# Latent attention in a two-layer decoder: the 64-row second part of the query products on two halves of TensorE's rows

## The reference

```python
q_latent = hidden_states @ Wqa                  # 256 -> 192
q = (q_latent @ Wqb).reshape(b, s, 16, 128)     # 64 plain + 64 rotary columns a head
q_pe, k_pe = rope(q_pe), rope(k_pe)
kv = (c_kv @ Wkvb)                              # c_kv has 64 columns
scores = einsum('bhqd,bhkd->bhqk', q_full, k_full) * scale   # causal
out = (softmax(scores) @ v) @ Wo
```

## Time and profile before

| | us |
|---|---|
| median of 3 runs | 822.75 (818.8 to 828.49) |
| the profiled execution | 815.32 |
| its span | 813.4 |
| PE busy | 623.1 (77%) |
| DVE busy | 469.7 (58%) |
| ACT busy | 320.4 (39%) |
| POOL busy | 254.9 (31%) |
| share of PE in the chain that ended last | 63% |
| mean granted TensorE clock | 0.88 |

### The profile page before, as it was taken

How to read it: one execution, slowest core, us unless ns; L and a number is a source line. 1 busy time by engine, 2 the same in 40 slices (tenths; PEclk the granted TensorE clock), 3 DMA queues, 4 the chain that set the end, 5 groups by cost and what they waited for, 6 DMA issues and landing times.

```text
span 813.4 us, 13142 instructions
## 1 busy us (share of the span) xinstructions
PE 623.1 (77%) x4335; PEld 435.4 (54%) x4338; DVE 469.7 (58%) x988; ACT 320.4 (39%) x754; POOL 254.9 (31%) x258
## 2 busy tenths in 40 slices
PE   3808899253099999999588998999988777763674
PEld 3408444142078888898473465556576356542332
DVE  4696699956445545555155153442546845878675
ACT  1501500242224333334242373553746435564444
POOL 3380178746500000000343892754903320100000
PEclk9958999755589999999868999999999878995778
DMA  9841000445541111110540000000000400000000
GB/s 321 293 161 47 1 0 1 155 155 179 192 135 41 52 52 52 52 40 26 162 125 0 1 1 0 0 0 0 0 2 1 155 1 2 2 2 1 6 19 26
DMA packets 35589, 50.01 MB, mean 61 GB/s; under 512 B 3288, under 2 KB 26400, under 8 KB 35296
## 3 DMA queue, kind: packets, MB, share of 16 engines
q1 hardware_dynamic: 33024, 41.39, 15.8%
q0 software_dynamic: 2528, 8.13, 2.7%
HBM read 38.50 MB, written 11.01 MB: 61 GB/s over the span
## 4 chain that ended last, share of the span: by engine, by line
PE 63%; DVE 18%; ACT 9%; POOL 4%; issue 3%; DMA 2%; SPq 0%; ACTq 0%; DVEq 0%; POOLq 0%
PE bank L1482 15%; PE bank L1495 5%; PE bank L1599 4%; PE bank L1598 4%; PE bank L1653 4%; POOL sorted_rows L472 3%; PE bank L1620 3%; DVE qk L898 2%; ACT sm L680 2%; PE bank L1370 2%; PE bank L1413 2%; PE bank L1414 2%; PE bank L1415 2%; PE bank L1612 2%; PE bank L1901 2%
## 5 line engine op out<-in xcount | busy, mean ns | idle before, releaser
L635 ACT ACTIVATE hf<-bank,be 128x256 f32<-128x256 f32 x120 | 50.4, 471 | 86.6 <-PE bank L1482 72.5
L1482 PE MATMUL bank<-h,wsp 128*128 128x256 f16 x720 | 81.3, 273 | 2.0 <-DVE h L1050 1.4
L1482 PEld LDWEIGHTS bank<-h,wsp 128*128 x720 | 69.5, 98 | 12.1 <-issue 3.7
L478 POOL DMA_INDIRECT yg<-expert_rows,pos x16 | 15.6, 977 | 185.8 <-DMA expert_rows<-yb 181.3
L1048 DVE CAST h<-hf 128x512 f16<-128x512 f32 x60 | 25.6, 427 | 65.2 <-ACT hf L635 63.7
L550 ACT CAST wsp<-wraw 128x2048 f16<-128x2048 f32 x12 | 22.6, 1897 | 73.0 <-DMA wraw<-in_L_ffn_W 73.0
L1151 DVE SCALAR_TENSOR_TENSOR sm<-bank,const 128x512 f32<-128x512 f32 x32 | 22.1, 692 | 50.1 <-PE bank L1620 50.1
L680 ACT ACTIVATE sm<-sm,nm 128x128 f32<-128x128 f32 x128 | 49.7, 393 | 1.0 <-DVE nm L1154 1.0
L460 POOL TENSOR_TENSOR kvp<-xnT,cxT 128x512 f32<-128x512 f32 x32 | 34.9, 1112 | 48.2 <-DVE xnT L877 40.2
L444 POOL TENSOR_TENSOR wsp<-wraw,wsp 128x2048 f16<-128x2048 f32 x10 | 40.9, 4095 | 10.8 <-ACT wsp L550 10.5
L488 POOL TENSOR_TENSOR rq<-qs,const 128x256 f32<-128x256 f32 x32 | 23.3, 728 | 65.2 <-ACT qs L686 65.1
(11 more groups left out here) (302 smaller groups left out, 1424.8 us busy)
## 6 DMA issues: line engine op xcount, KB each, us to landing
wraw<-in_L_ffn_W SPq DMA_DIRECT2D x16, 512.0 KB, 4.3
wraw<-in_L_ffn_W SPq DMA_DIRECT2D x8, 1024.0 KB, 5.5
sorted_rows<-early POOLq DMA_DIRECT2D x2, 1920.0 KB, 14.1
xg<-sorted_rows SPq DMA_DIRECT2D x15, 256.0 KB, 2.8
expert_rows<-yb SPq DMA_DIRECT2D x15, 256.0 KB, 2.2
tapR<-in_kpad SPq DMA_DIRECT2D x16, 128.0 KB, 6.9
x<-in_x SPq DMA_DIRECT2D x1, 1024.0 KB, 5.9
cx<-in_ctx SPq DMA_DIRECT2D x1, 1024.0 KB, 10.3
```

What stands on the lines that cost most here:

```text
L635: last = nc.scalar.activation(hf[:, p, SLOTS * k:SLOTS * k + SLOTS], bank[2 * (layer - 1) + p][:, SLOTS * k:SLOTS * k + SLOTS], ACT.Gelu, ...
L1482: last = nc.tensor.matmul(b[:, SLOTS * (f % 2):SLOTS * (f % 2) + SLOTS], w[a_][:, c, P * f:P * f + P], inp[:, b_, c, :], start=(c == 0 and ...
```

## The change

The second part of a query product (rows 128 to 192 of Wqb, 64 of TensorE's rows) is no longer made group by group. The latents' second half is computed twice over, into both halves of the partitions: `Wqa`'s last 64 columns are given twice by the host, `wqa` is 256 columns wide, and `ql1` has 128 partitions. The weights `wqb[:, 1]` hold the even groups in partitions 0 to 63 and the odd groups in 64 to 127. `queries_low` issues the 64-row products of two neighbouring groups one behind the other, on the two halves of the rows and into banks 1 and 2; they open the accumulation. `queries_high` issues the 128-row product of one group, which closes it and signals ACT. In the loop, step j now issues `queries_high` of group j-1, in odd steps preceded by `queries_low` of groups j-1 and j; group 7 is closed after the last scores. ACT's order, DVE's and POOL's are as before. The preparation follows the new places of the weights, and one more DMA brings them.

```diff
-        wqa = sb("wqa", [P, DC, QL], F32, s4w)
+        wqa = sb("wqa", [P, DC, 2 * P], F32, s4w)
...
-        ql1 = sb("ql1", [64, 2, P], F32, s4)
+        ql1 = sb("ql1", [P, 2, P], F32, s4)
...
-            sp.dma_start(wqb[0:64, 1].rearrange("p h n -> p (h n)"), a["L1_attn_Wqb"][P:QL, :]).then_inc(sem("w4_loaded"), 16)
+            for k in range(2):
+                sp.dma_start(wqb[64 * k:64 * k + 64, 1].rearrange("p (g two h) n -> p g two (h n)", two=2, h=4)[:, :, k],
+                             a["L1_attn_Wqb"][P:QL, :].rearrange("p (g two n) -> p g two n", two=2, n=4 * P)[:, :, k]).then_inc(sem("w4_loaded"), 16)
...
-                nc.scalar.copy(ql1[:].rearrange("p u s -> p (u s)"), bank[0][0:64, 2 * P:4 * P]).then_inc(sem("lat_copied"), 1)
+                nc.scalar.copy(ql1[:].rearrange("p u s -> p (u s)"), bank[0][:, 2 * P:4 * P]).then_inc(sem("lat_copied"), 1)
...
             for k in range(2):
+                half = slice(64 * k, 64 * k + 64)
                 for j in range(8):
-                    last = nc.tensor.transpose(bank[k][0:64, 64 * j:64 * j + 64], wqb[0:64, 1, 8 * k + j, 0:64], i64)
+                    last = nc.tensor.transpose(bank[k][0:64, 64 * j:64 * j + 64], wqb[half, 1, 8 * (j // 4) + 4 * k + j % 4, 0:64], ident[half, half])
...
-                for dst, w in ((bank[0][:, 0:2 * P], wqa[:, :, 0:P]), (bank[0][0:64, 2 * P:4 * P], wqa[:, :, P:QL])):
+                for dst, w in ((bank[0][:, 0:2 * P], wqa[:, :, 0:P]), (bank[0][:, 2 * P:4 * P], wqa[:, :, P:2 * P])):
...
-            def queries(i, j):
-                u, g = j // 4, j % 4
-                hs = slice(4 * g, 4 * g + 4)
+            def queries_low(i, j):
+
+                u = j // 4
                 if j == 0:
                     pe.wait_ge(sem("lat_copied"), i + 1)
-                pe.wait_ge(sem("q4_copied"), i * 8 + (j + 1))
-                nc.tensor.matmul(bank[1 + g % 2][:], ql0[:, u, :], wqb[:, 0, hs, :].rearrange("p h n -> p (h n)"), start=True, stop=False)
-                nc.tensor.matmul(bank[1 + g % 2][:], ql1[:, u, :], wqb[0:64, 1, hs, :].rearrange("p h n -> p (h n)"), start=False, stop=True).then_inc(sem("q4_psum"), 1)
+                pe.wait_ge(sem("q4_copied"), i * 8 + (j + 2))
+                for k in range(2):
+                    g, rows = (j + k) % 4, slice(64 * k, 64 * k + 64)
+                    nc.tensor.matmul(bank[1 + k][:], ql1[rows, u, :], wqb[rows, 1, 4 * g:4 * g + 4, :].rearrange("p h n -> p (h n)"), start=True, stop=False)
+
+            def queries_high(i, j):
+                u, g = j // 4, j % 4
+                nc.tensor.matmul(bank[1 + g % 2][:], ql0[:, u, :], wqb[:, 0, 4 * g:4 * g + 4, :].rearrange("p h n -> p (h n)"), start=False, stop=True).then_inc(sem("q4_psum"), 1)
...
                     scores(i, (j - 1) // 4, (j - 1) % 4)
                     if after is not None:
-                        if j == 1:
-                            queries(after, 0)
-                        queries(after, j)
+                        if j % 2:
+                            queries_low(after, j - 1)
+                        queries_high(after, j - 1)
                     if j >= 4:
                         turn_p(i, 0, j - 4)
                 scores(i, 1, 3)
+                if after is not None:
+                    queries_high(after, 7)
                 turn_p(i, 1, 0)
...
             latents(0)
-            queries(0, 0)
+            queries_low(0, 0)
+            queries_high(0, 0)
             key_latents(0, 0)
-            queries(0, 1)
+            queries_high(0, 1)
             turn_kv(0, 0)
-            for j in range(2, 5):
-                queries(0, j)
+            queries_low(0, 2)
+            queries_high(0, 2)
+            queries_high(0, 3)
+            queries_low(0, 4)
+            queries_high(0, 4)
             pe.wait_ge(sem("kvr_ready"), 1)
             key_latents(0, 1)
-            queries(0, 5)
+            queries_high(0, 5)
             turn_kv(0, 1)
-            for j in range(6, 8):
-                queries(0, j)
+            queries_low(0, 6)
+            queries_high(0, 6)
+            queries_high(0, 7)
...
+    wqa = inputs["L1_attn_Wqa"]
+    host["L1_attn_Wqa"] = np.ascontiguousarray(np.concatenate([wqa, wqa[:, P:]], 1))
```

More of the change, by code:

```diff
@@ L321, in prep4_moves @@
             for k in range(2):
-                yield wqbT[:, 8 * k:8 * k + 8, P:QL], bank[k][0:64, :].rearrange("p (h n) -> p h n", h=8)
+                yield (wqbT[:, :, P:QL].rearrange("p (g two h) n -> p g two h n", two=2, h=4)[:, :, k],
+                       bank[k][0:64, :].rearrange("p (g h n) -> p g h n", g=2, h=4))
             for k in range(2):
@@ L325, in prep4_moves @@
             for k in range(2):
-                yield wqb[0:64, 1, 8 * k:8 * k + 8, 0:64], bank[4 + k][0:64, :].rearrange("p (h n) -> p h n", h=8)
+                yield (wqb[64 * k:64 * k + 64, 1].rearrange("p (g two h) n -> p g two h n", two=2, h=4)[:, :, k, :, 0:64],
+                       bank[4 + k][64 * k:64 * k + 64, :].rearrange("p (g h n) -> p g h n", g=2, h=4))
             for k in range(4):
@@ L1523, in _ @@
             pe.wait_ge(sem("y_ready"), ET + CREDIT)
-            pe.wait_ge(sem("w4_loaded"), 96)
+            pe.wait_ge(sem("w4_loaded"), 112)
             def prep_copied(n):
@@ L1545, in _ @@
             for k in range(2):
+                half = slice(64 * k, 64 * k + 64)
                 for j in range(8):
-                    last = nc.tensor.transpose(bank[k][0:64, 64 * j:64 * j + 64], wqb[0:64, 1, 8 * k + j, 0:64], i64)
+                    last = nc.tensor.transpose(bank[k][0:64, 64 * j:64 * j + 64], wqb[half, 1, 8 * (j // 4) + 4 * k + j % 4, 0:64], ident[half, half])
                 last.then_inc(sem("prep4_psum"), 1)
             prep_copied(10)
[L1550 to L1555, removed]
+            for k in range(2):
+                for j in range(8):
+                    h = 8 * k + j
+                    last = nc.tensor.matmul(bank[2 + k][:, 64 * j:64 * j + 64], wqbT[:, h, 0:P], wkT[:, h, :], start=True, stop=True)
+                last.then_inc(sem("prep4_psum"), 1)
+            for k in range(2):
+                for j in range(8):
+                    h = 8 * (j // 4) + 4 * k + j % 4
+                    last = nc.tensor.matmul(bank[4 + k][64 * k:64 * k + 64, 64 * j:64 * j + 64], wqbT[:, h, P:QL], wkT[:, h, :], start=True, stop=True)
+                last.then_inc(sem("prep4_psum"), 1)
             pe.wait_ge(sem("wo4b_loaded"), 16)
```

## The result

The changed kernel takes **879.57 us** (median of 4 runs, 878.01 to 880.29) against 820.77 for the kernel before (4 runs, 818.58 to 828.49, the three of the prediction and one more beside the changed kernel): a ratio of 1.0707, 95% interval 1.0657 to 1.0756, some 58.8 us slower. The profiled execution took 879.73 us with a span of 877.8, which is 64.4 more than the span of 813.4 before.

The account below looks back on a forecast made before the run. PE was taken to bound the kernel, busy 46.1 of 48.35 us a pass. Waits +38, opening -3 and clock +20 made +55 on 815.3, 870.3; with a third of the distance to the median's 877.8, 873 us (846 to 896).

Parts of the forecast that it names:

- The waits, +38: Three loop passes: PE waits for ACT's copies, 2.87 us before turn_p in steps 4 to 7; +12.65 us a pass.
- The clock, +20: Loop passes: granted clock falls to 0.78 because of PE's waits, +6.8 us a pass.
- The sign that I had set, passes of 61 to 69 us: Loop passes: a pass of 61 to 69 us would show the forecast right, under 48 us wrong.
- The waits come, but the clock holds: Rival, loop passes: same waits without a lower clock, 850 to 858 us; chance 15%.
- The opening, -3: Opening of the latent attention: no exponentials there, so pairing gains; -3 us (-5 to -2).
- The pair at 0.86 plus switches: Two 64-row products side by side: 0.86 us, 1.25 with entry and exit in place of 2.40; 1.15 saved per pair.
- one by one: Rival, 64-row pairs: halves do not run side by side, 0.86 us more each, +13.8, 887 us; chance 5%.
- half an overlap: Rival, 64-row pairs: second product starts with the first's second pass, 1.29 us a pair, +7, 880 us; chance 8%.
- PE stays the bound: Rival, wait for qT at L1627: ACT copies qT(j) before qs(j-1) is ready; POOL caps the gain, 803 to 811 us; 6%.
- The preparation at "nothing": Preparation: one more DMA and eight 64-row transposes on the other half of the rows, costed at nothing.
- The base: Whole kernel before: profiled execution of 815.3 us, to which the terms were added; median 822.75 us, 7.4 higher.

Follow-up runs that it names:

- experiment 4: Changed kernel with ACT's exponentials of group j-2 put before its copy of the query products, PE untouched: 821.1 us, ratio 1.0116 to the kernel before.
- experiment 5: Changed kernel with added products whose result nobody uses filling PE's waits in steps 4 to 7: 850.4 us, ratio 1.0494 to the kernel before.
- experiment 3: Changed kernel with ACT's copy of the query products one step later, behind the next qT copy, PE untouched: 811.6 us, ratio 1.0016 to the kernel before.
- experiment 6: Kernel of experiment 2 with both 64-row products of a pair on partitions 0 to 63: 811.9 us, ratio 1.0007 to the kernel before.
- experiment 2: Changed kernel with PE's query products in the loop one step earlier, pairing kept: 801.6 us, ratio 0.9898 to the kernel before; repeated, 799.6 us, 0.9863.
- Experiment 8: Changed kernel with all 64-row weight transposes from rows 0 to 63: 870.1 us, ratio 1.0737 to the kernel before; beside it the changed kernel unedited, 867.7 us.
- The second group of runs: Changed kernel, unedited, timed again beside the kernel before on another chip: 867.7 us, ratio 1.0688.

## Why the prediction was right

It was 873 us (range 846 to 896, slower by more than 1% at 0.91), and the median is 879.57. Mechanism and place were right, not only the number; the size of the clock term was in part luck. Step by step:

- **The waits, +38.** Right in place, releaser and size. 2.87 us before turn_p was worked out and 2.79 is there; 2.43 before the scores of step 4 against 2.26, and 0.88 in steps 2 and 3 against 0.73. In all that is 14.9 us of waits in a pass (11.2 + 3.7), where 15.7 was put. To part waits from clock, I take PE's busy time at full clock from experiment 4: 42.64 + 42.64 + 40.82 = 126.1 in three passes. The changed kernel's is 148.2, so the clock cost it 22.1, and at full clock its passes would take, by this estimate, 204.1 - 22.1 = 182.0, that is +39.1. The second profile of the same kernel (passes of 210.5, PE busy 154.9) gives 210.5 - 28.8 = 181.7, +38.8. Forecast: 180.9. The passes of experiment 5, at 0.97 to 1.00, are 183.7 in all.
- **The clock, +20.** 22.1 and 28.8 in the two profiles, and some 16 by the ratios of experiment 5, whose clock of 0.97 is not quite whole in two of three passes. The level was nearly right: 0.78 was forecast for the stretch from the first scores to the last copy of query products, and the three passes of the first profile have 0.92, 0.76 and 0.85 there. The stretch takes 43.1, 49.0 and 45.6 us, where 39.8 + 6.8 was forecast. Whole passes, in both profiles, have 0.80 to 0.92. It is also the term that differs most between executions of one kernel: 0.92 and 0.85 in the first pass. That the sum fits so well owes something to luck. The forecast took the level of one other stretch, with waits of 1.98 us and 0.78, and experiment 3 shows that such waits do not fix it: up to 2.04 us, at 1.00, 0.97 and 0.93. The sign that I had set, passes of 61 to 69 us, held for two of the three (66.0, 71.8, 66.3). "The waits come, but the clock holds" is what experiment 4 looks like, with waits of 1.25, near the 1.23 that stood at a full clock in the earlier trace rows.
- **The opening, -3.** -3.0 measured.
- **The pair at 0.86 plus switches.** 1.06 to the product behind it and 0.19 more in that product, 1.07 in the chain against 0.88 without a pair ahead of it: 1.25, as forecast. The rivals "one by one" and "half an overlap" both fall with experiment 6: 1.91 is what one by one looks like, and half an overlap would be 1.29 and the switch. The Trainium skill ("TensorE: Matmul & The Clock Gate", Part 3, The mechanism) has matmuls start and end strictly in program order, and has those on different rows of the array overlap. The trace agrees with the overlap and does not contradict the order: the four records of the pair on two halves, in experiment 6, start in rising order, two by two, and end at 515.06, 515.07, 515.49 and 515.50. My prediction went wrong where it drew 1.29 from that rule and then set the trace against it; which record belongs to which product the trace does not say.
- **PE stays the bound.** Its place was right but its condition was not met. Moved a step (experiment 2) it comes true: POOL, named there, is indeed the next limit, and it caps the pass at 45.9, a gain of 2.4; up to 3 was forecast.
- **The preparation at "nothing".** In the first profile it was +12.7. Experiment 8 finds it in no other profile, the changed kernel's second one included, so the step stands; the cause of the 12.7 stays open.
- **The end of the kernel, not in the sum.** -6.0, with the clock at 0.85 in place of 0.80. In the profiles of the experiments this same code stands at 0.79 to 0.85 and takes 158.9 to 165.4 us, with no relation to the edit that I can see. Up to some 6 us of any comparison of single profiles here can be that.
- **The base.** 815.3 plus the measured terms, without the 12.7 of the preparation and the 6.0 of the end, is 815.3 + 61.1 - 3.0 = 873.4. The forecast of 873 is hence good by its own terms, and the last 6 us of 879.6 are two things that I had not foreseen and that partly cancel. The second group of runs, 867.7 against 813.2 on one chip, has +54.5, and the sum of the terms was +55.

## What to carry to other kernels

When work is moved by one step on one engine, write out the order of the engine that consumes it in the same step: a queue in order turns "one step later" into "behind everything that stood between", here 1.56 us of exponentials and a copy at each of four steps of a pass. Price a new wait twice, once as time and once as clock, and look whether waits of that length stand anywhere in the trace at a lower clock. A saving on PE that costs 7% in one order and gains 1% in another is worth keeping; move the handover on either side, and then relieve the engine that comes next.

## What the runs showed of the hardware

- Two float32 products of 64 rows and 512 columns on different halves of TensorE's rows, into different banks, ran fully side by side: 1.06 us for a pair with the switch ahead of it, 1.91 on one half.
- With waits of 2.79 us, four to a pass, the granted clock of a pass was 0.80 to 0.92; with 1.25 it was 1.00; with up to 2.04 (experiment 3) 0.93 to 1.00. Filling the waits with products that nobody uses brought it back to 0.97 to 1.00.
- Stalls without a releaser in the trace of one execution, here 7.96 us on ACT, can be of that execution alone: it stands in one of 13 profiles. A second profile of the same kernel tells this more cheaply than an experiment on a theory.
